# Sums over edge tiles in groups of four: accumulate in PSUM, then add once

## The reference

```python
def _hconv(x, src, dst, ew, w1, b1, w2, b2, g, b):
    h = jax.nn.relu(x @ w1 + b1)
    msg = ew[:, None] * h[src]
    agg = jax.ops.segment_sum(msg, dst, num_segments=x.shape[0])
    h = agg @ w2 + b2
    return jax.nn.relu(_bn(h, g, b))
```

## Time and profile before

| | us |
|---|---|
| median of 3 runs | 5181.58 (5176.66 to 5183.23) |
| span of the profiled execution | 7408.6 |
| its two stages of message sums (`sum_by_turns`) | 2956.1 and 2960.2 |
| GpSimd (POOL) busy | 3709.9 |
| TensorE (PE) busy | 3524.7 |
| VectorE (DVE) busy | 3079.5 |
| ScalarE (ACT) busy | 832.6 |

### The profile page before, as it was taken

How to read it: one execution, slowest core, us unless ns; L and a number is a source line. 1 busy time by engine, 2 the same in 40 slices (tenths; PEclk the granted TensorE clock), 3 DMA queues, 4 the chain that set the end, 5 groups by cost and what they waited for, 6 DMA issues and landing times. The chain is left out here.

```text
span 7408.6 us, 125636 instructions
## 1 busy us (share of the span) xinstructions
PE 3524.7 (48%) x20036; PEld 3259.3 (44%) x20037; DVE 3079.5 (42%) x9295; ACT 832.6 (11%) x1874; POOL 3709.9 (50%) x3766
## 2 busy tenths in 40 slices
PE   6344444433334444354444444343344343549999
PEld 5333333333334333354333333333333333438998
DVE  6333333333333333453333333333333335655665
ACT  4000000000000000130000000000000002444444
POOL 3544444444444444354444444444444442557777
PEclk9666666666666666676666666666666666559999
DMA  6222222222222222132222222222222222634444
GB/s 173 73 69 70 68 68 71 71 71 68 69 72 69 69 69 68 56 99 72 70 68 68 68 71 72 70 68 68 70 69 70 71 68 63 151 85 74 78 77 76
DMA packets 371980, 559.26 MB, mean 75 GB/s; under 512 B 137057, under 2 KB 266753, under 8 KB 371778
## 3 DMA queue, kind: packets, MB, share of 16 engines
q0 software_dynamic: 190848, 449.23, 23.1%
q1 hardware_dynamic: 141090, 87.80, 4.8%
q10 hardware_dynamic: 39968, 21.44, 1.1%
HBM read 477.60 MB, written 80.47 MB: 75 GB/s over the span
## 5 line engine op out<-in xcount | busy, mean ns | idle before, releaser
L858 POOL DMA_INDIRECT c_messages<-h,c_indices x2996 | 2833.2, 946 | 3071.9 <-DVE c_indices L938 2215.5
L905 PE MATMUL c_partial<-c_onehot,c_messages 128*128 128x128 f32 x12504 | 2273.5, 351 | 3509.4 <-issue 2159.8
L905 PEld LDWEIGHTS c_partial<-c_onehot,c_messages 128*128 128x128 f32 x12504 | 2096.5, 258 | 3682.8 <-issue 2321.5
L956 DVE TENSOR_TENSOR sums<-sums,c_partial 128x256 f32 x3126 | 1317.4, 421 | 3774.0 <-remote 2005.3
L923 DVE TENSOR_SCALAR c_onehot<-iota,edge_dst,edge_w 128x128 f32<-128x128 f32 x3136 | 1110.9, 355 | 0.1
L844 ACT ACTIVATE sums<-c_z,columns 128x192 f32 x256 | 93.6, 416 | 5819.8 <-issue 5819.8
L1884 POOL DMA_INDIRECT out<-ffn_result,ffn_table x210 | 335.7, 1599 | 97.1 <-issue 56.2
L1925 PE MATMUL ffn_ps<-ffn_xT,ffn_w_tile 128*128 128x256 f32 x1680 | 382.0, 381 | 0.0
L1925 PEld LDWEIGHTS ffn_ps<-ffn_xT,ffn_w_tile 128*128 128x128 f32 x1680 | 312.6, 191 | 38.5
L1568 POOL DMA_INDIRECT table<-rt_entry,rt_slot x196 | 187.8, 958 | 182.4 <-DVE rt_slot L1716 126.5
L1867 POOL DMA_INDIRECT ffn_rows<-tokens,ffn_table x218 | 231.8, 1064 | 67.9 <-issue 61.6
(11 more groups left out here) (189 smaller groups left out, 2492.2 us busy)
## 6 DMA issues: line engine op xcount, KB each, us to landing
c_messages<-h ACTq DMA_DIRECT2D x8320, 1.0 KB
c_messages<-h SPq DMA_DIRECT2D x8320, 1.0 KB
c_messages<-h,c_indices POOLq DMA_INDIRECT x2996
x<-in_x SPq DMA_DIRECT2D x28, 896.0 KB, 6.4
h<-pi_h ACTq DMA_DIRECT2D x14, 896.0 KB
out<-rt_x SPq DMA_DIRECT2D x14, 896.0 KB
tokens<-rt_tokens SPq DMA_DIRECT2D x14, 896.0 KB
h<-ph_h SPq DMA_DIRECT2D x24, 512.0 KB
```

What stands on the lines that cost most here:

```text
L858: pool.indirect_dma_start(messages[:, k, :], None, source, bass.IndirectOffsetOnAxis(ap=indices[:, k:k + 1], axis=0)).then_inc(s_message[k ...
L905: last = pe.matmul(partial[:, k % TURN_BANKS, g * P:(g + 1) * P], messages[:, slot, g * P:(g + 1) * P], onehot[:, k % TURN_ONEHOTS, :], st ...
L956: dve.tensor_tensor(where, where, partial[:, k % TURN_BANKS, 0:C].rearrange("p (g n) -> p g n", g=CG), ALU.add).then_inc(s_added, 1)
```

## The change

Four steps, a quad, share one first node, that of the quad's first tile. So their products can be added up in PSUM: the first step of a quad starts the accumulation and the last one ends it. VectorE adds once for each quad instead of once for each step. The two halves of the channels get a bank each, and three quads are held (6 banks) instead of four steps (4 banks). The node register is loaded for one quad at a time. The four onehot matrices of a later quad are built one after the other behind the quad's add. The copies of the row numbers come behind these builds: for half 0 behind the quad of steps 8 to 11, as before behind step 11, and for half 1 behind the quad of steps 20 to 23, where it was behind step 22. The waits on `s_added` count quads.

`plan_tiles` has to find the first node of each quad. GpSimd makes a 128x128 matrix `same_quad` that is 1 where the row is the first tile of the column's quad, and TensorE multiplies it with the first nodes of the tiles.

The gathers and the row DMAs stay as they are, as do the counts of matmuls and builds.

```diff
@@ -44,25 +44,28 @@
-TURN_BANKS = 4
+TURN_BANKS = 3
 TURN_ONEHOTS = 8
+QUAD = 4
+QUADS = TURN // QUAD
+ALL_QUADS = -(-EDGE_TILES // QUAD)
 TURNS = EDGE_TILES // TURN
...
 Z_AT = 12
-Z_PRODUCT = Z_AT + TURN_BANKS
-Z_STATS = Z_PRODUCT + 4
+Z_PRODUCT = Z_AT + QUAD
+Z_STATS = Z_PRODUCT + QUAD
@@ -140,9 +143,15 @@
+        same_quad = sb("same_quad", [P, P], F32)
+        quad_dst = sb("quad_dst", [P, K], F32)
         wide_tiles = ps("wide_tiles", [P, 512], F32)
+        quads = ps("quads", [P, 512], F32)
@@ -196,6 +205,13 @@
+            pool.memset(same_quad[:], 0.0).then_inc(s_same, 1)
+            pool.wait_ge(s_same, 1)
+            pool.affine_select(out=same_quad[:].rearrange("p (q f) -> p q f", f=QUAD),
+                               in_=same_quad[:].rearrange("p (q f) -> p q f", f=QUAD),
+                               compare_op=ALU.not_equal, fill=1.0, base=0,
+                               pattern=[[-QUAD, P // QUAD], [0, QUAD]], channel_multiplier=1).then_inc(s_same, 1)
+
@@ -223,15 +239,17 @@
             dve.memset(t["edge_dst"][:, EDGE_ROWS:], 0.0)
             dve.memset(t["edge_w"][:, EDGE_ROWS:], 0.0)
+            dve.wait_ge(s_rows[1], 16)
+            dve.tensor_copy(first_dst[:], g_dst[:, :, 0]).then_inc(s_first_dst, 1)
             dve.wait_ge(s_rows[0], 16)
             dve.tensor_copy(f_src[:], g_src[:]).then_inc(s_float[0], 1)
-            dve.wait_ge(s_rows[1], 16)
-            dve.tensor_copy(t["first_node"][:], g_dst[:, :, 0]).then_inc(s_first, 1)
-            link(dve.tensor_tensor(f_dst[:], g_dst[:], g_dst[:, :, 0:1].to_broadcast([P, K, P]), ALU.subtract))
+            dve.wait_ge(s_first_dst, 1)
+            dve.wait_ge(s_quads, 1)
+            dve.tensor_copy(t["first_node"][:], quads[:, 0:K]).then_inc(s_first, 1)
+            link(dve.tensor_copy(quad_dst[:], quads[:, 0:K]))
+            link(dve.tensor_tensor(f_dst[:], g_dst[:], quad_dst[:].unsqueeze(2).to_broadcast([P, K, P]), ALU.subtract))
             dve.tensor_scalar(exceeds[:], f_dst[:, :, P - 1], float(P), None, ALU.is_ge).then_inc(s_float[1], 1)
-
-            link(dve.tensor_copy(first_dst[:], g_dst[:, :, 0]))
             dve.wait_ge(s_iota, 4)
             link(dve.tensor_scalar(due[:], due_i[:], float((Z_CHUNKS - 1) * Z_COLS), None, ALU.min))
             link(dve.tensor_tensor(late[:], first_dst[:], due[:], ALU.is_lt))
@@ -255,6 +273,9 @@
+            pe.wait_ge(s_same, 2)
+            pe.wait_ge(s_first_dst, 1)
+            pe.matmul(quads[:, 0:K], same_quad[:], first_dst[:], start=True, stop=True).then_inc(s_quads, 1)
@@ -770,7 +791,7 @@
-        partial = ps("partial", [P, TURN_BANKS, 512], F32)
+        partial = ps("partial", [P, TURN_BANKS, CG, 512], F32)
@@ -830,7 +851,7 @@
-            sp.wait_ge(s_added, TURN_BANKS + EDGE_TILES)
+            sp.wait_ge(s_added, TURN_BANKS + ALL_QUADS)
@@ -874,7 +895,7 @@
             def product_of(chunk, turn):
-                pe.wait_ge(s_added, TURN_BANKS + Z_AT + turn * TURN)
+                pe.wait_ge(s_added, TURN_BANKS + Z_AT // QUAD + turn * QUADS)
                 if not isinstance(turn, int):
                     pe.wait_ge(s_z_stats, CG + chunk * CG)
@@ -890,21 +911,23 @@
                 for k in range(steps):
                     n = i * TURN + k
+                    quad, j = divmod(k, QUAD)
                     slot = FETCHED + place if k == FETCHED else k
                     if k == Z_PRODUCT and with_chunk:
                         product_of(i - 1, i)
+                    if j == 0:
+
+                        pe.wait_ge(s_added, i * QUADS + (quad + 1))
                     pe.wait_ge(s_onehot, n + 1)
-
-                    pe.wait_ge(s_added, n + 1)
                     if k == FETCHED:
                         for b in range(2):
                             pe.wait_ge(s_row[b][place], round_ * (16 * SHARE) + 16 * SHARE)
                     else:
                         pe.wait_ge(s_message[k], i * 16 + 16)
                     for g in range(CG):
-                        last = pe.matmul(partial[:, k % TURN_BANKS, g * P:(g + 1) * P],
+                        last = pe.matmul(partial[:, quad % TURN_BANKS, g, 0:P],
                                          messages[:, slot, g * P:(g + 1) * P], onehot[:, k % TURN_ONEHOTS, :],
-                                         start=True, stop=True)
+                                         start=(j == 0), stop=(j == QUAD - 1 or k == steps - 1))
                     last.then_inc(s_multiplied, 1)
             pe.sem_inc(s_multiplied, TURN)
@@ -930,7 +953,7 @@
                     dve.bn_stats(t["z_stats"][:, co, bass.ds(chunk, 1), :].rearrange("p a s -> p (a s)"),
                                  z[:, co, :]).then_inc(s_z_stats, 1)
-            regs = [dve.alloc_register(f"{name}_node{k}") for k in range(4)]
+            node_reg = dve.alloc_register(f"{name}_node")
             def copy_indices(turn, half):
@@ -940,28 +963,28 @@
             def turn_of(i, steps, with_chunk):
-                for k in range(steps):
-                    n = i * TURN + k
-                    if k == Z_STATS and with_chunk:
+                for quad in range(-(-steps // QUAD)):
+                    first, held = quad * QUAD, min(QUAD, steps - quad * QUAD)
+                    n = i * TURN + first
+                    if first == Z_STATS and with_chunk:
                         statistics(i - 1)
-                    if k % 4 == 0:
-
-                        dve.load(regs, t["step_nodes"][0:1, bass.ds(n, 4)])
-                        nodes = [dve.snap(r, min_val=0, max_val=NODES_PAD - 1) for r in regs]
-                    where = sums[:, :, bass.ds(nodes[k % 4], P)]
-
-                    dve.wait_ge(s_multiplied, TURN + n + 1)
-
-                    dve.wait_ge(s_added, TURN_BANKS + n)
+                    dve.load(node_reg, t["step_nodes"][0:1, bass.ds(n, 1)])
+                    node = dve.snap(node_reg, min_val=0, max_val=NODES_PAD - 1)
+                    where = sums[:, :, bass.ds(node, P)]
+
+                    dve.wait_ge(s_multiplied, n + (TURN + held))
+
+                    dve.wait_ge(s_added, i * QUADS + (TURN_BANKS + quad))
                     dve.tensor_tensor(where, where,
-                                      partial[:, k % TURN_BANKS, 0:C].rearrange("p (g n) -> p g n", g=CG),
+                                      partial[:, quad % TURN_BANKS, :, 0:P],
                                       ALU.add).then_inc(s_added, 1)
                     if steps < TURN:
                         continue
-                    build(k % TURN_ONEHOTS, n + TURN_ONEHOTS).then_inc(s_onehot, 1)
-
-                    for half, (first, end) in enumerate(HALVES):
-                        if k == end - 1:
+                    for j in range(QUAD):
+                        build((first + j) % TURN_ONEHOTS, n + (TURN_ONEHOTS + j)).then_inc(s_onehot, 1)
+
+                    for half, (_, end) in enumerate(HALVES):
+                        if first < end <= first + QUAD:
                             copy_indices(i + 1, half)
             for half in range(len(HALVES)):
```

More of the change, by code:

```diff
@@ L53 @@
 ROW_BYTES = C * 4
-assert TURN % TURN_BANKS == 0 and TURN % TURN_ONEHOTS == 0 and SHARE == 2 * ROW_BATCH
+assert TURN % QUAD == 0 and QUADS % TURN_BANKS == 0 and TURN % TURN_ONEHOTS == 0 and TURN_ONEHOTS % QUAD == 0 and SHARE == 2 * ROW_BATCH
 assert TURNS % 2 == 1
-assert 0 < STEPS_LEFT <= TURN_BANKS and STEPS_LEFT <= HALVES[0][1] and NODES_PAD * ROW_BYTES < 1 << 24
+assert 0 < STEPS_LEFT <= QUAD and STEPS_LEFT <= HALVES[0][1] and NODES_PAD * ROW_BYTES < 1 << 24
 ALL_ROUNDS = EDGE_ROWS // RING
@@ L62 @@
 Z_AT = 12
-Z_PRODUCT = Z_AT + TURN_BANKS
-Z_STATS = Z_PRODUCT + 4
-assert 0 < Z_REST <= Z_ROOM and Z_COLS <= Z_ROOM and Z_STATS < TURN
+Z_PRODUCT = Z_AT + QUAD
+Z_STATS = Z_PRODUCT + QUAD
+assert 0 < Z_REST <= Z_ROOM and Z_COLS <= Z_ROOM and Z_STATS < TURN and Z_AT % QUAD == 0
 COLS = 512
@@ L142, in plan_tiles @@
         f_dst = sb("f_dst", [P, K, P], F32)
+        same_quad = sb("same_quad", [P, P], F32)
+        quad_dst = sb("quad_dst", [P, K], F32)
         wide_tiles = ps("wide_tiles", [P, 512], F32)
+        quads = ps("quads", [P, 512], F32)
         turned = ps("turned", [P, 4, 512], F32)
+        s_same = sem("same")
+        s_first_dst = sem("first_dst")
+        s_quads = sem("quads")
         s_iota = sem("iota")
```

## The result

The changed kernel takes 5189.09 us (median of 20 runs, 5185.69 to 5193.39), the kernel before 5180.14 us beside it (20 runs). The ratio is 1.0017, with a 95% interval of 1.0010 to 1.0023: 9 us slower, inside the range and inside what was called no change, but clear of zero.

The account below looks back on a forecast made before the run. GpSimd's gathers were taken to bound the kernel, with other engines having room. All terms were 0 except +1.2 us for `plan_tiles`, so 5181.6 became 5183 us; the 8-in-10 range was 5168 to 5200 us.

Parts of the forecast that it names:

- what was called no change: Whole kernel: a move of at most about 0.2%, 10.4 us, taken as the least a measurement can tell; chance 0.84.
- The bound: Message sums: GpSimd's gathers bound at 28.8 us a turn and never wait in timed runs; saved VectorE adds worth 0.
- at most 1.231: Message sums: upper limit in us for a timed gather's period, from 5181.6 less 1492.3 for the other stages.
- I take this as the recording's doing: Profile before: GpSimd's 2215.5 us of index-copy waits were blamed on recording the gathers' traffic, so absent from timed runs.
- The builds and the port: VectorE beside GpSimd's gathers: four builds in a row cost 0, and sharing a port pair costs 0.
- Its rival: Port shared by VectorE and GpSimd: adds hold up gathers, so removing them gains, down to 4196 us; chance 0.01.
- `plan_tiles`: 1.2 us forecast: Planning stage: `src` conversion now behind the wait for `dst`, plus 13-column copies, adds 1.2 us; 0 to 1.8 possible.
- The index copies, onehots, rows: Message sums: later index copies, onehot builds and step 23's row DMAs all ready in time for GpSimd: 0.
- the 9.0 and 9.5 us of the sum: Message sums: how early the index copies for half 0 and half 1 come before GpSimd asks for them.
- The slower rival: Message sums: index waits are partly real, so delayed copies cost 2.9 us a turn, +380, 5560 us; chance 0.08.
- that wait in its sum: Half 1's index copy waiting for step 23's rows: rows just in time, copy with 9.5 us to spare: 0.
- The expectation that the profiled span could be some hundred us off: Changed kernel's profile: span some hundred us longer or shorter, as recording holds engines up elsewhere; timed runs decide.

Follow-up runs that it names:

- e1: The kernel before, unedited, profiled and timed again on a quick chip: 5175.95 us, ratio 0.9999 to the kernel before.
- e5: The changed kernel with each onehot matrix built twice, once into a buffer nothing reads, on a slow chip: 7817.98 us, ratio 1.0645 to the kernel before.
- e11: The changed kernel itself, unedited, run beside the kernel before on a slow chip: 7708.00 us, ratio 1.0494.
- e2: The kernel before with only the four onehot builds put in a row behind every fourth add, quick chip: 5184.78 us, ratio 1.0016.
- e4: The changed kernel with the builds reading the column numbers from PSUM instead of SBUF, quick chip: 5170.33 us, ratio 0.9990 to the kernel before.
- e3: The kernel before with only the new `plan_tiles`, message sums as before, quick chip: 5174.54 us, ratio 0.9996.

## Why the prediction was right, and where it wasn't

**The bound: right.** On a quick chip GpSimd's gathers follow one another without a wait, 0.946 and 0.30 us, as the sum had it; TensorE is at 74%, VectorE at 61% before and 42% after. The 965 us taken from VectorE were worth nothing. One number in this part was off: "at most 1.231" for a gather's period took the 1492.3 us of the other stages from the slow profile. In e1 these take about 1412 us (5174.5 less two message stages of 1881.3 from the first gather to the first weight load of `normalize_sums`), and the period is 1.2529.

**"I take this as the recording's doing": wrong.** The arithmetic before it was sound: 7408.6 less the index waits, against 5181.6, showed that the timed runs had no such waits. The cause given for the difference was a guess that nothing in the profile bore out. By it the waits should have stood in the changed kernel's profile again; there they are 51.7 us. e1 and e5 to e11 show what it was: chips of two kinds, and by all that the rows show the profile and the timed runs came from different ones. On a slow chip the waits of the earlier trace rows are real and are in the timed runs, too.

**The builds and the port: the term that failed, inside a forecast that came true.** The sum gave the new order of the builds 0 and asked only whether they were ready in time. For the port it looked at one gather beside two adds, found 0.94, and closed the matter, though its own sentence said that it is the builds that stay. Beside that very gather (2013.61 to 2014.55) lay a build, too, between the two adds, and it was the build that was slowed:

```profile
2014.13 0.47 DVE L923 TENSOR_SCALAR c_onehot<-iota,edge_dst,edge_w 128x128 f32<-128x128 f32 x1
```

0.47 us, where the median of that profile is 0.341 and its longest 0.579. Its rival was about the adds, with a gain as the sign. Measured: adds do nothing to a gather (945.3 ns on average beside an add alone, 945.5 beside nothing), builds do (956.2), four in a row more than single ones, +7.8 us here, +9.1 in e2. The range held because 9 us is small, not because this term was known. Set against e4, the builds cost the kernel before 2839.2 - 2832.3 = 6.9 us and the changed one 14.7. The page "SBUF — State Buffer" of the Trainium skill, section "SBUF: two separate sides", says that GpSimd can't write descriptors while VectorE runs an instruction in a two-port mode; "VectorE: DVE Perf Modes", section "Mode 2×_2P — use both read ports for one tensor", that this mode takes a single tensor source and needs SBUF. By these rules the build from SBUF falls under it, the one from PSUM and the add with its two tensors don't. The five kernels profiled on quick chips agree with that in sign. The size is small: the gathers at 1503.77 and 1521.40 lost 0.05 and 0.09 us beside builds of 1.11 us. The gathers of the trace on which the prediction rested could hardly show it (29 of 2996 take over 960 ns): there 1940 gathers have no work of VectorE's message sums beside them, 127 in e1.

**`plan_tiles`: 1.2 us forecast, 1.0 found.** From the first 13-column copy behind the wait for `dst` to the conversion of `iota`, both kernels on quick chips, first before, then changed:

```profile
9.38 0.18 DVE L229 COPY first_node<-pt_g_dst 128x13 int32<-128x13 int32 x1 [1.91 <-DMA pt_g_dst<-in_dst]
...
12.39 0.22 DVE L241 CAST iota<-iota_i 128x128 f32<-128x128 int32 x1
```

```profile
9.08 0.17 DVE L243 CAST pt_first_dst<-pt_g_dst 128x13 f32<-128x13 int32 x1 [8.10 <-DMA pt_g_dst<-in_dst]
9.17 1.02 DVE L245 CAST pt_f_src<-pt_g_src 128x1664 f32<-128x1664 int32 x1
9.37 0.50 PEld L278 LDWEIGHTS pt_quads<-pt_first_dst,pt_same_quad 128*128 128x128 f32 x2 [9.05 <-issue]
...
13.09 0.22 DVE L259 CAST iota<-iota_i 128x128 f32<-128x128 int32 x1
```

3.01 us have become 4.01; the little product lies beside the conversion, as said. But the 1.0 us can't be followed to the end of the stage: the first gather of all starts at 168.1 us in the changed kernel and 167.3 in e1, yet at 167.4 in e3 and 167.0 in e4, which both have the new `plan_tiles`. So 7.8 of the 9.0 us are shown; that `plan_tiles` makes up most of the rest is possible and not shown.

**The index copies, onehots, rows: right on a quick chip.** GpSimd doesn't wait, but the margins were smaller than the 9.0 and 9.5 us of the sum: from the end of the copy to the gather that needs it there are 7.1 us (half 0) and 6.6 (half 1) at the median in the changed kernel, and never less than 6.0. VectorE's busy time is 2186 us, where 2090 was said: that took the 3079.5 of the slow chip, and the quick one has 3151.5 before.

**The slower rival: it exists, and its price fits by luck.** It said 2.9 us a turn, +380 us, if the index waits were real. On the slow chips they are, and the change costs 7708.0 - 7345.2 = 363 us. But the terms were others. It put 2.13 us on the builds and 0.81 on the products of step 23; measured, half 1 waits 7.5 us longer, most of it for the rows of step 23, and half 0 waits 5.4 us less. The prediction had that wait in its sum, just in time and with 9.5 us to spare, and so at 0. Nor does the gather's period decide, as it said (0.946 + 0.30 there, too), but, as far as the rows show, whether the other engines work beside the gathers. The expectation that the profiled span could be some hundred us off for that reason was about the right thing under the wrong name.

## What to carry over

Before you read waits off a profile, see that its span agrees with the timed runs beside it; where it doesn't by more than a few per cent, it shows another regime, and a change must be judged in both (here 1.0017 and 1.0494). The same holds for a remedy: the builds from PSUM win on one kind of chip and cost 0.5% on the other. When one engine bounds, ask of every moved instruction not only whether it is ready in time but whether it disturbs that engine: 8 of the 9 us came from the order of builds that cost nothing by themselves. And release what the bounding engine waits for at the first moment at which it is free, behind the last product, not behind the add and the work that follow.

## What the runs showed of the hardware

A VectorE build with its tensor source and its result in SBUF and a GpSimd gather delay each other: gathers to 1.00 and 1.04 us from 0.946, builds to 583 ns from 341. The index copy, SBUF to SBUF as well, is delayed too (0.38 us from 0.17). With the build's source in PSUM neither is seen (builds 395 to 409 ns, gathers beside one 945.5 ns on average). An add of SBUF and PSUM doesn't delay a gather (945.3 ns).

The same program takes 5175 to 5182 us on some chips and 7344 to 7412 on others. In a stretch of 200 us far inside the first layer, with the gathers at the same 0.95 us, the slow chip of the first profile and the quick one of e1 read (length, busy us of PE, PEld, DVE, ACT, POOL with counts, clock, DMA share, GB/s):

```profile
1000.00:1200.00 200.00, 87.58 (x486) 82.29 (x487) 74.53 (x236) 2.92 (x8) 93.41 (x99) 0.66 0.24 69
```

```profile
1000.00:1200.00 200.00, 144.43 (x714) 127.31 (x715) 118.08 (x361) 5.12 (x14) 151.12 (x161) 0.73 0.39 109
```

On the slow chip the engines other than GpSimd are held up while gathers run: a register move of SyncE took 689 to 1386 ns there, and 29 to 38 ns in e1 (line 808, 1000 to 1100). What holds them is in no row, and no run here tells. It stays open, as does whether a chip stays of one kind.
